# A recurrent attention and gated feed-forward kernel: another way to build the mask, the block sums and the first transposed x in its setup

## The chip, the cores and the metric

The kernel runs on one core of a Trainium2 chip. The core has five engines that run side by side and wait for each other through semaphores: TensorE (PE, matrix products into PSUM), VectorE (DVE), ScalarE (ACT), GpSimd (POOL) and SyncE (SP, which here only issues transfers). The metric is the device time of one execution in microseconds, as a median of runs.

## The reference

x is [8, 1024, 512] in float32. With xn the layer norm of x over its last axis, the result is `x + s * silu(g)`.

- s is a recurrent attention. q = xn Wq; for i in 0 to 2, k = xn Wk[i], v = xn Wv[i], scores = (q kT) * w, where w[t, s] = sigmoid(decay_logits[i]) ** max(s - t - 1, 0) for s > t and 0 elsewhere; the three results (scores v) are blended with softmax(xn Wg), and go through Wo, times out_scale.
- g is a feed-forward net, silu(gate) * up and a product with down, whose three weight matrices (1376 x 512, 1376 x 512, 512 x 1376) are given as a table of 16 values and, for each weight, an index into it.

## The kernel before

**Numbers.** Each float32 operand of a matrix product is split in two float16 halves, high and low; a product takes three matmuls (high x high, high x low, low x high). The gate and up products use a scheme of seven products of sub-blocks in place of eight (Strassen's, in Winograd's form): it needs the sums S1 to S4 of sub-blocks of the weights and T1 to T4 of sub-blocks of the transposed x.

**Setup, and then a loop.** The setup turns the indices into weights, 33 units of 128 x 512 weights (`UNITS`). A unit b goes through these hands:

- POOL casts its codes to float16 in memory (L613, L618); SP loads them, each code row to four groups of partitions (L517).
- DVE compares them with the four candidates of its partition, 4 instructions of 128 x 2048 (L999), a one-hot matrix. It may be three units ahead of PE.
- PE looks up (`look_up`, L1371): 8 groups of 4 small matmuls, high and low half, into PSUM.
- ACT stores both halves as float16 (`store`, L761).

Behind its look-up, PE works through the unit's **pieces** (`PIECES`, `add_up`, `take_high`): a block sum is made in a PSUM bank by four matmuls of 512 columns with the identity or its negative (`plus`, `minus`; a high, a low, b high, b low). ACT copies the bank out as the high half (`store_sum`), PE subtracts this copy in the bank (one matmul, a unit later), and ACT copies what is left as the low half. The order of pieces is a table by units: for a set of blocks that begins at unit `BASE[s]`, S1 at +2 and +3, S3 at +3 and +4, S2 at +4 and +5, S4 at +6 and +7; T1 to T4 at units 26 to 31. Finished blocks of the weights are written to memory (`write_block`).

Between the units other setup work is placed by tables as well: the squares, high halves and low halves of the attention weights (`SQUARE_AT`, `HIGH_AT`, `LOW_AT`), where ACT makes a high half and DVE the low half from it (`low_part`, L1010); the norm and the normalized tiles of the first 512 rows of x (`XHAT_AT`, `XLOW_AT`); and their four transposes, which SP issues as DMA transposes at units 22, 23, 25 and 26 (`XPOSE_AT`, L498).

**The decay mask.** POOL raises the three decays to 128 powers, one per partition (L663), writes them with a row of zeros to a table in memory (L666, L668), and reads the table back, each partition one value further on (L670). PE turns the rows about with a product by a flip matrix (L1416), and ACT copies the outcome out of PSUM with its scale (L833). `mask` shares its memory with `eye4`, which DVE needs at the start.

The setup ends when PE has waited for the last piece, the low halves and the mask (L1584 to L1587). The loop then takes 16 groups of 512 rows: q and k (L1429), v, 42 sub-block products (L1541) with scores and retrieval between them, the down product (L1570), and the output. DVE combines the sub-block products (`u2` L1251, `c12` L1273 and others).

## Time and profile before

| | |
|---|---|
| median of 3 runs | 1888.74 us (1886.42 to 1889.11) |
| the profiled execution | 1886.13 us, its span in the profile 1884.3 us |
| granted TensorE clock | 0.996 of full speed |
| busy: PE, DVE, ACT, POOL | 1841.1, 1226.4, 648.9, 644.1 us |
| first matmul of the loop (L1429) | 144.4 us |
| chain that ended last | PE 94% |

The profile is of one execution. A line such as L1371 is a line of the kernel before, printed above. Matmuls overlap, so the start of one to the start of the next is what one costs; the duration shown is longer. In rows in order of time the figures are the start and the time until the last of the merged instructions ends, and what stands in brackets is how long the engine was idle before and which engine and line released it.

### The profile page before, as it was taken

How to read it: one execution, taken by the hardware profiler on the slowest of the kernel's cores; microseconds unless marked ns; L12 is line 12 of the kernel's file. 1: busy time of each engine (PE TensorE's matmuls, PEld its weight loads, DVE VectorE, ACT ScalarE, POOL GpSimd, SP SyncE). 2: the span in 40 equal slices, each digit the busy share in tenths (PEclk: the TensorE clock that was granted, in tenths of full speed). 3: DMA queues.
4: the chain of work that ended last, by engine and by line, in shares of the span. 5: the costliest groups of instructions: out<-in, count | busy, mean ns of one | idle time of the engine just before them, and what ended most of it. 6: DMA issues, size and time to landing. Idle time of an engine off the chain costs nothing.

```text
span 1884.3 us, 39423 instructions
## 1 busy us (share of the span) xinstructions
PE 1841.1 (98%) x14198; PEld 1249.3 (66%) x14198; DVE 1226.4 (65%) x2565; ACT 648.9 (34%) x1168; POOL 644.1 (34%) x642
## 2 busy tenths in 40 slices
PE   5889999999999999999999999999999999999999
PEld 1236758486776848576685858667584867758485
DVE  7785848485674848576584847658484856748374
ACT  2564324242333414233342324233242424334131
POOL 9301606043250605234160613416061432506021
PEclk9999999999999999999999999999999999999999
DMA  9974737465563736566472655548363655737350
GB/s 216 312 219 135 186 87 184 103 162 135 149 168 102 199 84 163 132 159 153 111 198 78 172 133 153 142 128 193 82 176 113 161 139 139 178 96 198 68 141 26
DMA packets 353020, 276.73 MB, mean 147 GB/s; under 512 B 220349, under 2 KB 257600, under 8 KB 352752
## 3 DMA queue, kind: packets, MB, share of 16 engines
q1 hardware_dynamic: 341888, 267.61, 54.4%
q0 software_dynamic: 10944, 6.50, 2.4%
q8 instruction: 132, 2.16, 0.4%
q14 instruction: 56, 0.46, 0.1%
HBM read 204.16 MB, written 30.54 MB: 125 GB/s over the span
## 4 chain that ended last, share of the span: by engine, by line
PE 94%; DVE 1%; SPq 1%; ACT 1%; POOL 1%; DMA 1%; issue 1%; another core or an unknown queue 0%; POOLq 0%; DVEq 0%
PE F L1541 43%; PE F L1570 24%; PE B L1429 16%; PE B L1461 2%; PE B L1434 2%; PE B L1436 2%; PE B L1435 2%; DVE region L999 1%; PE F L1371 1%; POOL codes L613 1%; PE F L1434 1%; PE F L1435 1%; PE F L1436 1%; DMA region<-in_wv 1%; SPq L517 0%
## 5 line engine op out<-in xcount | busy, mean ns | idle before, releaser
L1541 PE MATMUL F<-xtc,ring 128*128 128x256 f16 (+1 forms) x4224 | 497.7, 273 | 0.0
L1541 PEld LDWEIGHTS F<-xtc,ring 128*128 128x128 f16 (+1 forms) x4224 | 416.0, 100 | 42.4
L1570 PE MATMUL F<-wd_hi,region 128*128 128x512 f16 (+1 forms) x1408 | 429.2, 379 | 0.0
L1541 PE MATMUL F<-xt,ring 128*128 128x256 f16 (+1 forms) x3168 | 378.8, 273 | 0.1
L1541 PEld LDWEIGHTS F<-xt,ring 128*128 128x128 f16 (+1 forms) x3168 | 310.0, 100 | 35.7 <-DVE region L1261 1.8
L1570 PE MATMUL F<-wd_lo,region 128*128 128x512 f16 (+1 forms) x704 | 266.7, 379 | 0.0
L1570 PEld LDWEIGHTS F<-wd_hi,region 128*128 128x128 f16 (+1 forms) x1408 | 137.6, 98 | 162.6
L1345 DVE SCALAR_TENSOR_TENSOR region<-F,row_out,region 128x512 f32<-128x512 f32 x64 | 48.0, 751 | 291.3 <-ACT region L926 291.3
L680 POOL TENSOR_TENSOR rstd<-var,nhalf 128x4 f32<-128x4 f32 x15 | 15.1, 1008 | 638.1 <-DVE var L957 638.1
L686 POOL TENSOR_TENSOR region<-region 128x512 f16<-128x512 f32 x96 | 121.7, 1267 | 220.8 <-ACT region L761 220.8
L926 ACT ACTIVATE region<-F,scale_hf 128x512 f32<-128x512 f32 x64 | 44.0, 687 | 435.6 <-PE F L1570 435.6
L761 ACT ACTIVATE region<-region 128x512 f16<-128x512 f32 x192 | 113.7, 592 | 138.8 <-DVE region L1293 105.6
L1429 PE MATMUL B<-xt,a_hi 128*128 128x512 f16 x512 | 154.6, 382 | 4.3 <-issue 3.0
L698 POOL TENSOR_TENSOR region<-faded,region 128x384 f16<-128x384 f32 x64 | 69.5, 1086 | 226.7 <-ACT region L761 226.7
L1222 DVE SCALAR_TENSOR_TENSOR region<-B,region 128x512 f16<-128x512 f32 x64 | 44.2, 691 | 134.6 <-ACT region L761 134.6
L1429 PE MATMUL B<-a_hi,xt 128*128 128x387 f16 x512 | 128.7, 328 | 0.0
L874 ACT ACTIVATE region<-F,scale_down 128x512 f32<-128x512 f32 x96 | 62.2, 648 | 186.9 <-POOL region L693 126.9
L1570 PEld LDWEIGHTS F<-wd_lo,region 128*128 128x128 f16 (+1 forms) x704 | 68.9, 98 | 79.5
L693 POOL TENSOR_TENSOR region<-region 128x512 f16<-128x512 f32 x96 | 103.0, 1073 | 24.5 <-ACT region L761 24.5
L761 ACT ACTIVATE region<-B 128x512 f16<-128x512 f32 (+1 forms) x128 | 68.7, 536 | 110.5 <-PE B L1429 110.5
L1251 DVE TENSOR_TENSOR region<-F,region 128x512 f32<-128x512 f32 x96 | 61.7, 643 | 66.7 <-PE F L1541 56.5
L1436 PE MATMUL B<-region 128*128 128x128 f16 x552 | 99.0, 219 | 0.0
(197 smaller groups left out, 2955.4 us busy)
## 6 DMA issues: line engine op xcount, KB each, us to landing
ring<-blocks SPq DMA_DIRECT2D x546, 256.0 KB, 3.1
x_sb<-in_x SPq DMA_DIRECT2D x64, 256.0 KB, 3.5
out_y<-x_sb SPq DMA_DIRECT2D x64, 256.0 KB, 2.0
ring<-blocks SPq DMA_DIRECT2D x112, 128.0 KB, 2.5
blocks<-ring SPq DMA_DIRECT2D x35, 256.0 KB, 6.0
x_sb<-codes SPq DMA_DIRECT2D x10, 512.0 KB, 8.0
chalf<-codes SPq DMA_DIRECT2D x9, 512.0 KB, 8.2
xt<-codes SPq DMA_DIRECT2D x9, 512.0 KB, 9.6
```

Of the source, the lines that this page charges most:

```text
L686: G_.tensor_tensor(h_lo[0:M, ms, 0:HALF], XC[s % 2][0:M, 0:w], h_hi[0:M, ms, 0:HALF], ALU.subtract).then_inc(s_hl1, 1)
L693: G_.tensor_tensor(h_lo[0:M, ms, HALF:GRP], SC[0:M, 0:w], h_hi[0:M, ms, HALF:GRP], ALU.subtract).then_inc(s_hl2, 1)
L698: G_.tensor_tensor(pr_half[:, 1], probs[:, :], pr_half[:, 0], ALU.subtract).then_inc(s_prl, 1)
L761: return nc.scalar.activation(dst, src, ACT.Copy, **kw)
L874: nc.scalar.activation(SC[0:M, 0:w], pair(0, s), ACT.Silu, scale=f_down[0:M, LUT:LUT + 1]).then_inc(s_sg1, 1)
L1251: V_.tensor_tensor(xc, pair(1, s), xc, ALU.add).then_inc(s_u2, 1)
L1429: ins = T_.matmul(bank[0:M, 0:cols], a, b, start=(n == 0), stop=(n == 3 * len(pairs) - 1))
L1434: T_.matmul(out, ah, bh, start=True, stop=False)
L1435: T_.matmul(out, ah, bl, start=False, stop=False)
L1436: return T_.matmul(out, al, bh, start=False, stop=True)
L1541: ins = T_.matmul(out_, a, b, start=fresh, stop=False, skip_group_check=True)
L1570: ins = T_.matmul(bf[:, :], a, b, start=(k == 0 and n == 0), stop=(k == FC - 1 and n == 2))
```

## The change

- **Mask.** The flip matrix, the table in memory and its three transfers, PE's product and ACT's copy are gone. POOL makes the mask in place: an iota of s - t - 1, a maximum with 0, a power of the decays, a select that keeps s > t, and a product with the scale, each over 3 x 128 columns and each waiting for the one before.
- **Block sums.** S2, S4, T2 and T4 start from what the bank still holds. After `take_high` that is the low half of the sum before; one matmul adds its high half again, and two add the other block. S4 and T2 have the opposite sign of before, so `u2` and `c12` subtract the product where they added it. Each set's S1, S2 and S4 now share one of two banks; S3 has a third; x and the T sums have the fourth.
- **First x.** Each tile of the first 512 rows is transposed on PE, 4 matmuls of 128 columns against `plus` per half, and copied out by ACT; these are pieces of units 15 to 22. SP's four DMA transposes are gone. T1, T2, T4, T3 come at units 23, 25, 27 and 29.
- **Low halves.** `LOW_AT` puts DVE's low halves at units 23, 25, 26, 28 and 30; the high halves stay at 19, 21, 22, 24 and 26.

```diff
--- before.py
+++ after.py
@@ -106,32 +106,38 @@
-    SUM = {S1: (A21, 1, A22), S3: (A11, -1, A21), S2: (S1, -1, A11), S4: (A12, -1, S2)}
-    SUMT = {T1: ("B12", "B11"), T3: ("B22", "B12"), T2: ("B22", T1), T4: ("B21", T2)}
-    BANK_OF = {S1: 0, S2: 1, S3: 2, S4: 3}
-    BANK_OFT = {T1: 0, T2: 1, T3: 2, T4: 3}
...
+    SUM = {S1: (A21, 1, A22), S3: (A11, -1, A21), S2: (S1, -1, A11), S4: (S2, -1, A12)}
+    SUMT = {T1: ("B12", -1, "B11"), T3: ("B22", -1, "B12"), T2: (T1, -1, "B22"), T4: (T2, 1, "B21")}
+    CHAINED = (S2, S4)
+    CHAINEDT = (T2, T4)
...
-    q = BASE[SETS[-2]]
-    for op, a in ((T1, 4), (T3, 5), (T2, 6), (T4, 8)):
-        PIECES.setdefault(q + a, []).append((None, op, 0))
-        PIECES.setdefault(q + a + 1, []).append((None, op, 1))
+    for op, u in ((T1, 23), (T2, 25), (T4, 27), (T3, 29)):
+        PIECES.setdefault(u, []).append((None, op, 0))
+        PIECES.setdefault(u + 1, []).append((None, op, 1))
+    for j, u in enumerate((15, 17, 19, 21)):
+        PIECES.setdefault(u, []).append(("x", j, 0))
+        PIECES.setdefault(u + 1, []).append(("x", j, 1))
...
+    def bank_of(s, op):
+        if s is None or s == "x":
+            return 3
+        return 2 if op == S3 else SETS.index(s) % 2
...
-        bank = (BANK_OFT if s is None else BANK_OF)[op]
-        if part == 0:
-            BUSY[s, op] = before.get(bank, 0)
-        else:
-            before[bank] = n + 1
+        BUSY[s, op, part] = before.get(bank_of(s, op), 0)
+        before[bank_of(s, op)] = n + 1
@@ -434,14 +435,13 @@
-        LOW_AT = {20: 0, 22: 1, 23: 2, 25: 3, 27: WO}
+        LOW_AT = {23: 0, 25: 1, 26: 2, 28: 3, 30: WO}
...
-        XPOSE_AT = {22: 0, 23: 1, 25: 2, 26: 3}
@@ -531,8 +533,6 @@
-                if b in XPOSE_AT:
-                    transpose_x(0, XPOSE_AT[b], XPOSE_AT[b] + 1)
@@ -620,16 +620,12 @@
-            G_.memset(flip[:, :], 0.0).then_inc(s_cstep, 1)
...
-            G_.memset(fade_end, 0.0).then_inc(s_cstep, 1)
...
-            pool.wait_ge(s_cstep, 6)
+            pool.wait_ge(s_cstep, 4)
...
-            G_.affine_select(out=flip[:, :], in_=flip[:, :], compare_op=ALU.not_equal, fill=1.0,
-                             base=-(P - 1), pattern=[[1, P]], channel_multiplier=1).then_inc(s_const, 1)
@@ -658,16 +654,24 @@
-            pool.wait_ge(s_cstep, 9)
+            pool.wait_ge(s_cstep, 7)
...
-            with nc.allow_non_contiguous_dma(reason="384 values, once"):
-                pool.dma_start(fade_rows[:, P:2 * P], fade_end).then_inc(s_row, 16)
-                pool.wait_ge(s_pow, 1)
-                pool.dma_start(fade_rows[:, 0:P].rearrange("h t -> t h"), fade_t[:, :]).then_inc(s_row, 16)
-                pool.wait_ge(s_row, 32)
-                pool.dma_start(mask_up[:, :, :], bass.AP(fade_rows, 1, [[1, P], [2 * P, NH], [1, P]])).then_inc(s_mrow, 16)
...
+            band = dict(pattern=[[0, NH], [-1, P]], base=-1, channel_multiplier=1)
+            G_.iota(mask_up, allow_small_or_imprecise_dtypes=True, **band).then_inc(s_mstep, 1)
+            pool.wait_ge(s_mstep, 1)
+            G_.tensor_scalar(mask_up, mask_up, 0.0, None, ALU.max).then_inc(s_mstep, 1)
+            pool.wait_ge(s_mstep, 2)
+            pool.wait_ge(s_pick, 2 * CG)
+            G_.tensor_tensor(mask[:, :, :], decay[:, :].unsqueeze(2).broadcast_to([P, NH, P]), mask_up,
+                             ALU.pow).then_inc(s_mstep, 1)
+            pool.wait_ge(s_mstep, 3)
+            G_.affine_select(out=mask[:, :, :], in_=mask[:, :, :], compare_op=ALU.is_ge, fill=0.0,
+                             **band).then_inc(s_mstep, 1)
+            pool.wait_ge(s_mstep, 4)
+            G_.tensor_scalar(mask[:, :, :], mask[:, :, :], 2.0 ** SP, None, ALU.mult).then_inc(s_mask, 1)
@@ -717,9 +721,9 @@
-                    G_.tensor_tensor(tt[:, T2], b22, tt[:, T1], ALU.subtract).then_inc(s_tt, 1)
+                    G_.tensor_tensor(tt[:, T2], tt[:, T1], b22, ALU.subtract).then_inc(s_tt, 1)
...
-                    G_.tensor_tensor(tt[:, T4], b21, tt[:, T2], ALU.subtract).then_inc(s_tt, 1)
+                    G_.tensor_tensor(tt[:, T4], b21, tt[:, T2], ALU.add).then_inc(s_tt, 1)
@@ -818,20 +822,21 @@
-                if s is None:
-                    copy(held(s, op, part), B[BANK_OFT[op]][:, :].rearrange("p (k t) -> p k t", k=2)).then_inc(s_sum, 1)
+                bank = B[bank_of(s, op)]
+                if s == "x":
+                    t = TILES[op]
+                    copy(xt[:, 0, part * KC:(part + 1) * KC, t * P:(t + 1) * P],
+                         bank[:, :].rearrange("p (k t) -> p k t", k=KC)).then_inc(s_sum, 1)
+                elif s is None:
+                    copy(held(s, op, part), bank[:, :].rearrange("p (k t) -> p k t", k=2)).then_inc(s_sum, 1)
...
-                    copy(held(s, op, part), B[BANK_OF[op]][:, 0:width(s)]).then_inc(s_sum, 1)
+                    copy(held(s, op, part), bank[:, 0:width(s)]).then_inc(s_sum, 1)
...
-                if b == NU - 1:
-                    act.wait_ge(s_pmask, 1)
-                    copy(mask[:, :, :].rearrange("p h t -> p (h t)"), LUHI[NU % 2][:, 0:HD],
-                         scale=2.0 ** SP).then_inc(s_mask, 1)
@@ -1248,7 +1253,7 @@
-                    V_.tensor_tensor(xc, pair(1, s), xc, ALU.add).then_inc(s_u2, 1)
+                    V_.tensor_tensor(xc, xc, pair(1, s), ALU.subtract).then_inc(s_u2, 1)
@@ -1270,7 +1275,7 @@
-                    V_.tensor_tensor(YC[0:M, 0:w], pair(3, s), YC[0:M, 0:w], ALU.add).then_inc(s_c12, 1)
+                    V_.tensor_tensor(YC[0:M, 0:w], YC[0:M, 0:w], pair(3, s), ALU.subtract).then_inc(s_c12, 1)
@@ -1383,40 +1387,49 @@
-                if s is None:
-                    (a, b), sign, bank = SUMT[op], -1, B[BANK_OFT[op]][:, :]
-                else:
-                    a, sign, b = SUM[op]
-                    bank = B[BANK_OF[op]][:, 0:width(s)]
-                if BUSY[s, op]:
-                    pe.wait_ge(s_sum, BUSY[s, op])
+                a, sign, b = (SUMT if s is None else SUM)[op]
+                bank = B[bank_of(s, op)][:, :] if s is None else B[bank_of(s, op)][:, 0:width(s)]
+                if BUSY[s, op, 0]:
+                    pe.wait_ge(s_sum, BUSY[s, op, 0])
...
-                T_.matmul(bank, plus[:, :], held(s, a, 0), start=True, stop=False)
-                T_.matmul(bank, plus[:, :], held(s, a, 1), start=False, stop=False)
-                T_.matmul(bank, other[:, :], held(s, b, 0), start=False, stop=False)
-                T_.matmul(bank, other[:, :], held(s, b, 1), start=False, stop=True).then_inc(s_psum, 1)
+                if op in (CHAINEDT if s is None else CHAINED):
+                    T_.matmul(bank, plus[:, :], held(s, a, 0), start=False, stop=False, skip_group_check=True)
+                else:
+                    T_.matmul(bank, plus[:, :], held(s, a, 0), start=True, stop=False, skip_group_check=True)
+                    T_.matmul(bank, plus[:, :], held(s, a, 1), start=False, stop=False, skip_group_check=True)
+                T_.matmul(bank, other[:, :], held(s, b, 0), start=False, stop=False, skip_group_check=True)
+                T_.matmul(bank, other[:, :], held(s, b, 1), start=False, stop=True,
+                          skip_group_check=True).then_inc(s_psum, 1)
...
-                bank = B[BANK_OFT[op]][:, :] if s is None else B[BANK_OF[op]][:, 0:width(s)]
+                bank = B[bank_of(s, op)][:, :] if s is None else B[bank_of(s, op)][:, 0:width(s)]
...
+            def turn_x(j, hl):
...
+                bank = B[bank_of("x", j)]
+                if BUSY["x", j, hl]:
+                    pe.wait_ge(s_sum, BUSY["x", j, hl])
+                pe.wait_ge(s_xlo, j + 1)
+                for k in range(KC):
+                    ins = T_.matmul(bank[:, k * P:(k + 1) * P], xhat_half[:, TILES[j], hl, k * P:(k + 1) * P],
+                                    plus[:, :], start=True, stop=True, skip_group_check=True)
+                ins.then_inc(s_psum, 1)
...
-                if b == NU - 1:
-                    pe.wait_ge(s_mrow, 16)
-                    pe.wait_ge(s_wst, STORED[NU - 2])
-                    T_.matmul(LUHI[NU % 2][:, 0:HD], flip[:, :], mask_up.rearrange("p h t -> p (h t)"),
-                              start=True, stop=True).then_inc(s_pmask, 1)
...
-                    if part == 0:
+                    if s == "x":
+                        turn_x(op, part)
+                    elif part == 0:
@@ -1481,7 +1494,7 @@
-                    pe.wait_ge(s_xt[t], 16 * (gi + 1))
+                    pe.wait_ge(s_xt[t], 16 * (gi + FREE))
```

## Rows read from the trace of the kernel before

**Rows 1.** The page, part 1: busy time by engine
```profile
PE 1841.1 (98%) x14198; PEld 1249.3 (66%) x14198; DVE 1226.4 (65%) x2565; ACT 648.9 (34%) x1168; POOL 644.1 (34%) x642
```

**Rows 2.** The chain that ended last, in order of time: start us, us, what
```profile
6.89 13.96 POOL codes L613 x20
...
62.77 0.43 PE B L1396
...
111.40 0.22 PE B L1396
...
144.36 20.13 PE B L1429 x96
```

**Rows 3.** PE in order of time (start us, us), first matmuls of some look-ups
```profile
88.35 0.40 PE L1371 MATMUL F<-region,pick_hi 128*32 128x512 f16 x4 [1.17 <-DVE region L999]
...
91.97 0.40 PE L1371 MATMUL F<-region,pick_hi 128*32 128x512 f16 x4
...
95.19 0.40 PE L1371 MATMUL F<-region,pick_hi 128*32 128x512 f16 x4
...
98.81 0.40 PE L1371 MATMUL F<-region,pick_hi 128*32 128x512 f16 x4
...
103.94 0.62 PE L1371 MATMUL F<-region,pick_hi 128*32 128x512 f16 x4 [2.89 <-ACT tt L761]
...
108.57 0.40 PE L1371 MATMUL F<-region,pick_hi 128*32 128x512 f16 x4 [0.31 <-ACT ring L761]
...
112.20 0.40 PE L1371 MATMUL F<-region,pick_hi 128*32 128x512 f16 x4
...
136.88 0.40 PE L1371 MATMUL F<-region,pick_hi 128*32 128x512 f16 x4
...
138.72 0.91 PE L1416 MATMUL F<-faded,mixed 128*128 128x384 f32 x2
```

**Rows 4.** DVE in order of time: a compare (L999), low halves (L1010)
```profile
90.10 2.85 DVE L999 TENSOR_SCALAR region<-xt,code 128x2048 f16<-128x2048 f16 x4
...
93.62 0.76 DVE L1010 SCALAR_TENSOR_TENSOR a_lo<-region,scale_up,a_hi 128x512 f16<-128x512 f32 x1 [0.67 <-ACT a_hi L761]
...
101.31 1.82 DVE L1010 SCALAR_TENSOR_TENSOR a_lo<-region,scale_up,a_hi 128x1536 f16<-128x1536 f32 x1 [1.63 <-issue]
```

**Rows 5.** ACT in order of time, around unit 21 and at the end
```profile
99.67 1.60 ACT L761 ACTIVATE a_hi<-region,scale_up 128x1536 f16<-128x1536 f32 x1
...
139.91 0.53 ACT L761 ACTIVATE mask<-F 128x384 f32<-128x384 f32 x1
...
140.28 0.65 ACT L761 ACTIVATE ring<-B 128x512 f16<-128x512 f32 x1
```

**Rows 6.** PE's matmuls of 128 columns (168 us), then SyncE's queue (93 us)
```profile
168.40 0.22 PE L1434 MATMUL B<-region 128*128 128x128 f16 x1
...
168.85 0.22 PE L1436 MATMUL B<-region 128*128 128x128 f16 x1
...
93.69 9.60 SPq L498 DMA_TRANSPOSE xt<-xhat_half  x1
```

**Rows 7.** POOL in order of time, setup
```profile
5.03 0.29 POOL L631 TENSOR_SCALAR_AFFINE_SELECT mixed<-mixed 128x128 f32<-128x128 f32 x1
...
84.80 0.77 POOL L655 IOTA fade_s<- 128x3 f32 x1 [8.03 <-issue]
...
87.74 1.17 POOL L663 TENSOR_TENSOR fade_tile<-decay,fade_tile 128x3 f32<-128x3 f32 x1
```

**Rows 8.** Lines by themselves: duration ns min/median/max, first and last start us, forms
```profile
L680 POOL TENSOR_TENSOR rstd<-var,nhalf x15: 1006/1007/1029, 161.2 to 1679.3; 128x4 f32<-128x4 f32 x15
...
L703 POOL TENSOR_TENSOR faded<-state,fade_tile x56: 825/827/1157, 173.2 to 1831.7; 128x384 f32<-128x384 f32 x56
...
L999 DVE TENSOR_SCALAR region<-x_sb,code x1: 748/748/748, 88.1 to 88.1; 128x2048 f16<-128x2048 f16 x1
...
L1286 DVE SCALAR_TENSOR_TENSOR region<-region,scale_hf x96: 480/752/1716, 175.1 to 1848.7; 128x512 f32<-128x512 f32 x80, 96x256 f32<-96x256 f32 x16
```

More of the change, by code:

```diff
@@ L189, in attention_ffn_kernel @@
         fade_s = sb("fade_s", [P, NH], F32)
-        flip = mixed
-        fade_end = mask[0:NH, 1]
-        fade_rows = nc.dram_tensor("fade_rows", [NH, 2 * P], F32, kind="Internal")
         codes16 = nc.dram_tensor("codes16", [NU, QR, CG * BANK], F16, kind="Internal")
@@ L324, in attention_ffn_kernel @@
         s_pick = sem("pick_ready")
-        s_row = sem("fade_rows_written")
-        s_mrow = sem("mask_rows_in")
-        s_pmask = sem("mask_in_psum")
+        s_mstep = sem("mask_step")
         s_mask = sem("mask_ready")
@@ L474, in _ @@
             sp.sem_inc(s_xtc, 32 * FREE)
+            for t in range(GT):
+                sp.sem_inc(s_xt[t], 16 * FREE)
             sp.dma_start(lutrow[:, :], lut.partition_broadcast(P)).then_inc(s_small, 16)
@@ L1039, in shifted @@
                 V_.tensor_scalar(dst, src, 23, None, ALU.logical_shift_left).then_inc(done, 1)
-            dve.wait_ge(s_const, 3)
+            dve.wait_ge(s_const, 2)
             step(V_.tensor_reduce(eye[:, :], eye4.rearrange("p a c -> p c a"), AX.X, ALU.add))
@@ L1376, in ready @@
                 if s is None and op not in SUMT:
-                    for t in range(GT):
-                        pe.wait_ge(s_xt[t], 16)
+                    pe.wait_ge(s_sum, NTH["x", GT - 1, 1] + 1)
                 elif (s, op) in HELD:
```

## The prediction

> **What bounds the kernel now.** I read the page first: PE is busy 98% of the span [rows 1], so a stage gets shorter only where PE waits or does less. The chain of waits, in order of time, splits the span in two. It begins on POOL, which issues the code casts, and up to 144.36 us it passes through several engines. From there on it is PE's matmuls of the main loop [rows 2]. The change edits the setup; in the loop it only swaps operands and signs. So I price the 144.4 us of setup and let the rest shift with it.
>
> PE's instructions in order of time say where the setup can give. A unit (one look-up and its pieces) starts with the first L1371 matmul. From unit 25 to unit 32 PE takes 112.20 to 136.88 = 24.68 us for 7 units with 50 matmuls of 512 columns (pieces of units 25 to 31 by the old table) [rows 3]. An add costs 0.216 us at full clock [rows 2], so 24.68 - 50 x 0.216 leaves 1.98 us for a look-up with its gaps. There PE sets the pace. Units 20 to 24, started at 91.97, 95.19, 98.81, 103.94 and 108.57 and ended at 112.20, have 5, 5, 1, 4 and 5 such matmuls. At PE's pace they would take 3.06, 3.06, 2.20, 2.84 and 3.06; they took 3.22, 3.62, 5.13, 4.63 and 3.63. The excess is 0.16 + 0.56 + 2.93 + 1.79 + 0.57 = 6.0 us. The DVE rows name its cause: the low half of matrix 0 stands 0.67 us idle for ACT's high half. That of matrix 1 starts at 101.31 after 1.63 us idle, just as ACT's high half of it ends (99.67 + 1.60 = 101.27) [rows 4, 5]. The compare of unit 23 is queued behind this 1.82 us instruction, and PE's look-up 23 stands 2.89 us idle (put down to ACT, but its one-hots are what is late). It then restarts with matmuls of 0.62 instead of 0.40 us, TensorE at 1.2 instead of 2.4 GHz [rows 3].
>
> **Low halves four units behind.** The same five DVE instructions, now at units 23, 25, 26, 28 and 30. ACT has finished each high half over one unit before. Nothing waits, so DVE starts compare 21 at 92.95 instead of after the low half of matrix 0 (93.62 + 0.76), and what PE then sees late is nothing: PE's own pace takes over. This returns the 6.0 us. DVE needs 2.65 us a compare (its 2.85 for four overlap by about 0.2), PE 1.98 plus its pieces. With my new piece counts DVE stays ahead by 0.8 us at its closest, unit 27, after both 1.7 us low halves. If that lead were gone, each us of DVE delay would cost one.
>
> **Chained sums.** S2, S4, T2 and T4 lose one matmul each: 140 become 126, 14 in all. Units 20 to 31 go from 70 to 63 (T moved forward within them): 7 x 0.216 = 1.5 us. One more lies in unit 11, at half clock, on the chain: 0.43 [rows 2]; I take 0.4. Those of earlier units stand in waits for codes, and cost and give nothing. S4 in the tail is counted below. The loop's two DVE subtractions have the shape and length of the adds they replace; their second operand is now in PSUM, which no row shows. As PE is the loop's bound, I take 0, bounds -1 to +3 us.
>
> **First x on TensorE.** Added: 8 pieces of 4 matmuls of 128 columns at units 15 to 22, and 8 ACT copies of about half a us. From 168.40 to 168.85 eight such matmuls follow each other in 0.45: 0.056 each [rows 6]. In units 15 to 18 PE waits for DVE anyhow. In 19 to 22 there are 16: 0.9 us. ACT gets 0.5 us more a unit and its two 1.6 us high halves fall in units 21 and 22, so PE's T1 and S4 pieces meet it about 0.3 us early: -0.3. Removed: four DMA transposes. The longest holds SyncE's queue 9.60 us [rows 6], with code loads and block writes behind it; but the idle times of DVE after 61 us end on ACT and not on codes, so it gives 0 (bounds 0 to 1). The Trainium skill (TensorE: Matmul & The Clock Gate, Part 4: PE-mode transpose) has such a transpose at about 275 ns in a kernel; by it 16 of them would be 4.4 us and not 0.9, a gain 3.5 us smaller. The rows above are for ordinary matmuls against an identity, which these are, so I keep 0.056.
>
> **Mask, what goes.** On POOL a memset and a select for the flip matrix (0.29 for the select [rows 7]) and a small memset, 0.5 us in all ahead of the casts that start the chain. DMA sets the pace soon after: 0.3, bounds 0 to 0.5. At the end, ACT's copy of the mask: the next copy starts 0.37 later (139.91 to 140.28) [rows 5], plus one matmul of S4, 0.22: 0.6 us. PE's mask matmul (at 138.72) lies beside ACT's stores.
>
> **Mask, what comes.** Five POOL instructions over 384 columns after the small powers, from about 88.9 us (87.74 + 1.17 [rows 7]). Four are simple. A select of 128 columns takes 0.29, a product of 384 columns 0.83 [rows 7, 8]: 1.2 to 3.3 us, I take 2.3. Do they hold DVE? A POOL iota of three columns started at 84.80 and took 0.77, to about the end of a compare: one engine does wait for the other. In the loop the DVE line L1286 runs 0.75 us as a rule and 1.72 at most, beside POOL [rows 8]. So I charge 2.3 less the 0.8 of DVE lead: 1.5, bounds 0 to 3.3. The power itself no row shows at this size. Below: 0.83, the product of the same shape. Above: 1.007 us for 4 columns [rows 8] is 0.25 a column, x 384 = 97 us. Three columns took 1.17 against 1.007 for four [rows 7, 8], so a fixed part is large; I take the geometric middle, 9 us. As to what it holds: the compare at 88.1 ran its usual 748 ns inside the power of 87.74 to 88.91 [rows 7, 8]. So I let it hold nothing. It ends near 100, and the mask is wanted only by the loop at about 138.
>
> The Trainium skill (SBUF — State Buffer, Who interferes with whom) says that a DVE instruction in a two-port mode and a GpSimd instruction exclude each other, and that the one issued first has the ports to its end. The 0.77 us iota agrees, the compare inside the power doesn't; by the rule DVE would also stand still for the whole power.
>
> **Sum.** 6.0 + 1.5 - 0.9 - 0.3 = 6.3 for units 19 to 32; + 0.4 + 0.3 + 0.6 - 1.5 = 6.1 us. The loop would start at 138.3 instead of 144.36. The profiled execution took 1886.1 (span 1884.3); less 6.1 is 1880.0. The median of the runs before, 1888.7, is 2.6 above that execution, so I forecast 1882.6.
>
> **Rivals.** (1) The power of 384 columns sets the end. If it holds the ports for its length P, each us of P costs one, and the change is slower than before from P = 6.1. At my 9 us it is 1882.6 + 9 = 1891.6, with PE's restart at half clock about 1893. If it holds nothing but is slow, the mask comes at 91.2 + P, late from P = 47; at 97 the loop starts at 188 and the time is near 1933. For it: the stretched DVE line, and four columns that cost 1.007. Against: the undisturbed compare, and little growth from three to four columns. 0.27. The page's rule is this rival.
> (2) The wait moves and does not go. ACT carries 8 copies more just where its long high halves lie, POOL's simple instructions cost the full 3.3, the 0.7 of the early stages stay hidden, and half of the 6.0 comes back as PE waits: 6.1 - 1.8 - 0.7 - 3.0 = 0.6, time 1888.1. For it: ACT's 1.60 us halves at units 21 and 22. Against: ACT is idle ahead of most of its stores. 0.17.
> (3) The forecast, 0.56, own range 1879.5 to 1885: all savings in full (0.2 + 0.2 more), POOL free (1.5 more) and 1 us for spread at the low end; 1.8 for POOL at 3.3 and some ACT at the high.
>
> **Numbers.** Below 0.2% (3.8 us) a measurement of this kernel can't tell a change from none. The forecast case is faster nearly always (0.55), and 0.03 comes from cases between it and rival 2; the rest of 2 is no change, 0.15. Rival 1 is slower, 0.27. Range: from 1879 up to 1895, which leaves out the long powers.
>
> **What would show it.** Right: the first L1429 at about 138; no idle of PE over 1 us and no matmuls at half clock between units 19 and 32; compares 20 to 23 back to back. DVE's compares at 0.75 us each beside POOL's power; a power under 40 us. Wrong: compares stretched to the length of a POOL instruction (rival 1), or a first L1429 that waits on POOL; ACT named ahead of PE's pieces of units 23 and 24 (rival 2); and a loop that isn't 1740 us long (1884.3 - 144.4), which none of my terms has.

## The result: slower by 0.4%, and one GpSimd instruction has it

The kernel before took 1888.92 us (median of 6 runs, 1886.42 to 1890.11), the changed kernel 1895.38 us (6 runs, 1894.83 to 1898.36): ratio 1.0038, 95% interval 1.0025 to 1.0051. The forecast was 1882.6 us, faster. The second case of rival 1, a power that holds (almost) nothing but is slow, is what happened, with 62 us instead of my 9.

The page of the changed kernel, part 1 (answers to [rows 1]): POOL is busy 62.6 us longer, PE 4 us less.

```profile
PE 1837.0 (97%) x14214; PEld 1249.3 (66%) x14214; DVE 1227.0 (65%) x2565; ACT 652.1 (34%) x1175; POOL 706.7 (37%) x641
```

The chain of waits, in order of time (answers to [rows 2]): POOL stands alone on it from 91.88 on, and the loop starts 12.1 us later than before.

```profile
91.88 61.88 POOL mask L668
156.46 20.08 PE B L1442 x96
```

POOL's instructions in order of time (start us, us), answering to [rows 7]. The power of 384 columns takes 61.87 us; the iota, the maximum, the select and the product around it take 1.03, 1.71, 0.53 and 1.21.

```profile
87.82 1.17 POOL L659 TENSOR_TENSOR fade_tile<-decay,fade_tile 128x3 f32<-128x3 f32 x1
88.96 1.03 POOL L663 IOTA faded<- 128x384 f32 x1
90.09 1.71 POOL L665 TENSOR_SCALAR faded<-faded 128x384 f32<-128x384 f32 x1
91.88 61.87 POOL L668 TENSOR_TENSOR mask<-decay,faded 128x384 f32<-128x384 f32 x1
153.81 0.53 POOL L671 TENSOR_SCALAR_AFFINE_SELECT mask<-mask 128x384 f32<-128x384 f32 x1
154.43 1.21 POOL L674 TENSOR_SCALAR mask<-mask 128x384 f32<-128x384 f32 x1
```

PE's instructions in order of time (answers to [rows 3]; idle time and releaser in brackets). After unit 19's first look-up (88.43) PE is idle only 0.31 us (for DVE, at 90.59) and 0.21 us (for ACT, at 103.78) until the tail; the 2.89 us hole and the half clock behind it are gone. The last two steps of the tail start at 134.98 and 136.48, and then PE stands 19.59 us for the mask.

```profile
88.43 0.40 PE L1376 MATMUL F<-region,pick_hi 128*32 128x512 f16 x4 [1.16 <-DVE region L1004]
...
134.98 0.38 PE L1398 MATMUL B<-ring,plus 128*128 128x512 f16 x1 [1.53 <-ACT ring L765]
...
136.48 0.39 PE L1410 MATMUL B<-ring,minus 128*128 128x512 f16 x1 [0.69 <-ACT ring L765]
...
156.46 1.03 PE L1442 MATMUL B<-xt,a_hi 128*128 128x512 f16 x2 [19.59 <-POOL mask L674]
```

In every kernel here the loop's first matmul, where the mask doesn't hold it, comes 1.57 to 1.82 us after that last one-matmul step (1.57 before, 142.79 to 144.36). Without the wait it would have come at 136.48 + 1.57 = 138.05, or up to 0.25 later.

DVE's instructions in order of time (answers to [rows 4]). The low halves stand without idle time. Four compares that end beside the iota took 3.01 and the next eight 6.42; further into the power eight take 5.38. One by one, the usual compare takes 0.75; the one beside the iota took 1.02, the two beside the maximum 0.98 each, and the first one that begins inside the power 1.31, which is the row of 92.26 (from the same view of a narrower stretch).

```profile
87.53 3.01 DVE L1004 TENSOR_SCALAR region<-x_sb,code 128x2048 f16<-128x2048 f16 x4
90.46 6.42 DVE L1004 TENSOR_SCALAR region<-xt,code 128x2048 f16<-128x2048 f16 x8
...
92.26 1.31 DVE L1004 TENSOR_SCALAR region<-xt,code 128x2048 f16<-128x2048 f16 x1
...
96.80 5.38 DVE L1004 TENSOR_SCALAR region<-chalf,code 128x2048 f16<-128x2048 f16 x8
102.10 0.75 DVE L1015 SCALAR_TENSOR_TENSOR a_lo<-region,scale_up,a_hi 128x512 f16<-128x512 f32 x1
102.76 5.38 DVE L1004 TENSOR_SCALAR region<-x_sb,code 128x2048 f16<-128x2048 f16 x8
108.06 1.81 DVE L1015 SCALAR_TENSOR_TENSOR a_lo<-region,scale_up,a_hi 128x1536 f16<-128x1536 f32 x1
```

The account between the two profiled executions: the start goes from 144.36 to 156.46, +12.1 us; the loop (span less start) from 1884.3 - 144.4 = 1739.9 to 1893.2 - 156.5 = 1736.7, -3.2 us. Together +8.9, the difference of the spans; the medians differ by 6.5.

**A mark behind the noisy part.** Everything ahead of unit 19 shifts as a block from execution to execution: its first look-up started anywhere from 88.04 to 91.02. So starts are compared below by their *distance*: the time from that look-up to the loop's first matmul. Two executions of one kernel (e4 and e12 below) give 48.77 and 48.79, though the starts themselves are 138.69 and 137.85. All distances come from one profiled execution per kernel, so these two are the whole measure of their spread, beside e3, which adds only GpSimd work to the kernel before and gives 55.88 against 56.01. Before it is 144.36 - 88.35 = 56.01; after, without the mask's wait, 138.05 - 88.43 = 49.62.

### The profile page after: what moved, and what is told of

It reads as the page before. It is cut to its first block, busy times and chain, and to the rows that moved or that the text cites. A ratio compares the mean times of both kernels' runs of the same rounds, so it can differ in the third digit from the quotient of the medians.

```text
span 1893.2 us, 39454 instructions
## 1 busy us (share of the span) xinstructions
PE 1837.0 (97%) x14214; PEld 1249.3 (66%) x14214; DVE 1227.0 (65%) x2565; ACT 652.1 (34%) x1175; POOL 706.7 (37%) x641
## 4 chain that ended last, share of the span: by engine, by line
PE 92%; POOL 4%; DVE 1%; DMA 1%; issue 1%; SPq 1%; ACT 1%; POOLq 0%; DVEq 0%
PE F L1554 43%; PE F L1583 24%; PE B L1442 16%; POOL mask L668 3%; PE B L1474 2%; PE B L1447 2%; PE B L1449 2%; PE B L1448 2%; DVE region L1004 1%; PE F L1447 1%; PE F L1448 1%; PE F L1449 1%; DMA region<-in_wv 1%; SPq L519 0%; DMA lutrow<-in_lut 0%
## 5 line engine op out<-in xcount | busy, mean ns | idle before, releaser
L1256 DVE TENSOR_TENSOR region<-region,F 128x512 f32<-128x512 f32 x96 | 61.4, 640 | 66.6 <-PE F L1554 56.5
L1442 PEld LDWEIGHTS B<-xt,a_hi 128*128 128x128 f16 x512 | 49.8, 98 | 83.0 <-issue 24.8
```

The lines of the kernel that those rows point to most:

```text
L1256: V_.tensor_tensor(xc, xc, pair(1, s), ALU.subtract).then_inc(s_u2, 1)
L1442: ins = T_.matmul(bank[0:M, 0:cols], a, b, start=(n == 0), stop=(n == 3 * len(pairs) - 1))
```

## The experiments

Ratios are to the kernel before on the same chip, with 95% intervals.

**e1: the change with the old mask** (the memory table, flip matrix, TensorE matmul and ACT copy put back; everything else as after).

```
- G_.tensor_tensor(mask, decay broadcast, mask_up, ALU.pow)
...
+ pool.dma_start(fade_rows[:, 0:P].rearrange("h t -> t h"), fade_t)
...
+ T_.matmul(LUHI[NU % 2][:, 0:HD], flip, mask_up)
+ copy(mask, LUHI[NU % 2][:, 0:HD], scale=2.0 ** SP)
```

> The changed kernel with the mask of the kernel before put back (flip matrix, table in memory, PE product, ACT copy); chained sums, first x on TensorE and the late low halves stay. Theory: POOL's power over 384 columns (61.9 us in the profile after) is the whole loss, and the rest of the change gives what was forecast. Then PE, whose last setup matmul of the profile after ended near 137, starts the loop at 138 to 139 us instead of 144.4, and the time is 5 to 8 us below before (ratio 0.9960 to 0.9975). Rival: the 19.6 us wait for the mask hides another loss (first transposed x late, block writes late, ACT behind); then the loop starts after 141 us and the ratio is 0.999 or more.

Measured 1882.32 us, ratio 0.9972 (0.9962 to 0.9983). So the loss sits in the mask, as the theory has it. But the loop started at 142.59 and not at 138 to 139, as the rival has it (its ratio did not come); the distance is 53.24, 4.5 us more than the factored mask of e4 gives. 0.4 of it lies in the tail, where the mask's matmul and copy stand: from unit 32's first look-up to the loop 7.22 us pass here and 6.83 in e4. The other 4.3 lie in units 22 and 23. PE's instructions with idle time in front, between 99 and 111 us, show most of these: 0.39 + 0.21 + 0.78 + 1.65 = 3.0 us in which PE stood, mostly for nothing that the profile shows.

```profile
100.70 0.38 PE L1382 MATMUL F<-region,pick_hi 128*32 128x512 f16 x1 [0.39 <-issue]
101.28 0.42 PE L1382 MATMUL F<-region,pick_hi 128*32 128x512 f16 x2 [0.21 <-issue]
103.56 0.39 PE L1416 MATMUL B<-ring,minus 128*128 128x512 f16 x1 [0.78 <-ACT ring L767]
106.63 0.40 PE L1382 MATMUL F<-region,pick_lo 128*32 128x512 f16 x3 [1.65 <-issue]
```

ACT, in order of time, stands there too, and again no engine or transfer of the kernel is named.

```profile
101.44 0.60 ACT L767 ACTIVATE wd_hi<-F 128x512 f16<-128x512 f32 x1 [3.72 <-remote]
```

**e2: the kernel before with GpSimd's mask only.**

```
- the table's three DMAs, the flip matmul and the ACT copy
+ iota, maximum, power of 384 columns, select, product on GpSimd
```

> The kernel before with the mask made on POOL and nothing else of the change. Theory (the power alone loses): the power takes 61 to 63 us, the loop starts at 155 to 157 us, 11 to 13 us later than before. The loop of the changed kernel was 3 us shorter than before (1736.7 against 1739.9 us). If that comes from the two DVE subtractions or the x sums, this loop is 1740 us long and the ratio 1.006; if it comes from the late start or is chance, it may be 1737 here too, ratio 1.0045. Rival: the power is slow only beside the new order of compares; then it is clearly off 62 us here.

1898.89 us, ratio 1.0059 (1.0044 to 1.0075); the loop starts at 158.89. POOL in order of time:

```profile
94.47 61.86 POOL L662 TENSOR_TENSOR mask<-decay,faded 128x384 f32<-128x384 f32 x1
156.40 0.53 POOL L665 TENSOR_SCALAR_AFFINE_SELECT mask<-mask 128x384 f32<-128x384 f32 x1
```

The mask edit alone makes the kernel slower. The power took the same 61.86 us, and the first compare inside it again 1.31. The loop was 1738.2 us long. The start is 2 us later than I expected because the whole setup was (unit 19 at 91.02).

**e3: powers of several sizes**, added to the kernel before on GpSimd behind its table: 24 and 96 columns with exponents up to 31, 96 columns with exponent 1, the same once more when DVE is done, and a product of 96 columns.

> The kernel before with POOL powers added after its mask table is read, where POOL is idle: 24 columns, 96 columns with exponents 0 to 31, 96 columns with all exponents 1, and, once DVE has ended its setup, 96 columns again and a product of 96 columns. The added results are not used. Theory (own arithmetic, about 0.16 us a column over a fixed part of about 0.4): 4.2, 15.8, 15.8, 15.8 us, and under 0.6 us for the product. Rival 1 (POOL and DVE share ports and the power fights the compares): the power beside an idle DVE is far shorter, under 5 us. Rival 2 (the cost hangs on the exponents): with exponents of 1 it is under half of that with 0 to 31.

1886.36 us (one run). POOL in order of time; x2 groups the 24 with the first 96, and the two later 96.

```profile
102.23 20.67 POOL L680 TENSOR_TENSOR probe_o<-decay,probe_e 128x24 f32<-128x24 f32 x2
...
123.64 31.70 POOL L680 TENSOR_TENSOR probe_o<-decay,probe_e 128x96 f32<-128x96 f32 x2
155.42 0.35 POOL L692 TENSOR_TENSOR probe_o<-decay,probe_e 128x96 f32<-128x96 f32 x1
```

Line L680 by itself (duration ns min/median/max) gives the ends of the range:

```profile
L680 POOL TENSOR_TENSOR probe_o<-decay,probe_e x4: 4680/15761/15942, 102.2 to 139.7; 128x96 f32<-128x96 f32 x3, 128x24 f32<-128x24 f32 x1
```

24 columns take 4.68 us; 96 take 15.91 with exponents up to 31, 15.94 with exponent 1, and 15.62 when DVE is idle for the first 9.9 us of it (it has four short instructions in the rest). (15.91 - 4.68) / 72 = 0.156 us a column, and (61.87 - 15.91) / 288 = 0.160 from there to 384. In these runs the price is linear in the columns, with under 1 us fixed, and neither the exponent nor DVE's work moves it by more than 0.4 us. A product of 96 columns takes 0.35: the power is over 45 times that.

**e4: the change with a factored mask.** Each decay's power of an exponent is a product of a coarse, a fine and a row power: 8 + 16 + 1 columns for each of 3 decays, 75 in all instead of 384, made on GpSimd ahead of its all-reduce, where it is idle.

```
...
+ G_.tensor_tensor(powers, decay broadcast, powers, ALU.pow)          # 75 columns
...
+ G_.tensor_tensor(coarse(mask_up), powers 8 broadcast, powers 16 broadcast, ALU.mult)
+ G_.tensor_tensor(mask, mask_up, powers 1 broadcast, ALU.mult)
+ G_.affine_select(out=mask, in_=mask, compare_op=ALU.is_ge, fill=0.0)
```

> The changed kernel with the mask factored: powers of 8, 16 and 1 columns for each decay (75 columns in one instruction), two products of 384 columns and a select, on POOL between the code casts and the sum over partitions, where it stood idle 21 us. Theory (0.16 us a column): the power takes 12 to 13 us, the mask is ready near 72 us, the sum over partitions is hardly later, and the loop starts at 137.5 to 138.5 us: 6 to 8 us below before, and equal to or up to 1 us better than with the table put back. Rival (a fixed cost dominates the power or POOL's work holds DVE): the power takes over 20 us or compares are stretched, the sum over partitions comes late, and the loop starts after 141 us.

1876.95 us, ratio 0.9944 (0.9931 to 0.9958); the loop starts at 138.69. This beats both kernels: 11 us under the one before, of which 7.2 are the shorter distance (56.01 to 48.77) and 3.8 a shorter loop (1739.9 to 1736.1), which no edit to the loop explains (see there below). Run again as e12:

> The kernel with the factored mask once more, as it was, to stand beside the other three on the same chip: ratio 0.994 to 0.995 as measured (0.9944), loop start at 138 to 139.5, loop 1736 to 1737 us long. If the loop's start or length moves by 2 us or more between two executions of one kernel, then differences of that size between single profiles say nothing.

1876.91 us, ratio 0.9938 (0.9925 to 0.9952), loop start 137.85, loop 1736.95 us long. POOL in order of time in e12: 12.32 us for 75 columns (0.164 a column; up to 15.29 in its other variants, 0.204 a column, for which I have no cause), and the mask is ready at 71.9, 66 us ahead of need.

```profile
55.72 12.32 POOL L664 TENSOR_TENSOR powers<-decay,powers 128x75 f32<-128x75 f32 x1 [0.15 <-POOL powers L660]
68.14 0.95 POOL L667 TENSOR_SCALAR powers<-powers 128x3 f32<-128x3 f32 x1
68.48 1.28 POOL L669 TENSOR_TENSOR faded<-powers 128x384 f32<-128x384 f32 x1
69.83 1.16 POOL L674 TENSOR_TENSOR mask<-faded,powers 128x384 f32<-128x384 f32 x1
71.07 0.86 POOL L677 TENSOR_SCALAR_AFFINE_SELECT mask<-mask 128x384 f32<-128x384 f32 x1
```

**e7: e4 with the low halves at their old units**, which prices that item.

```
- LOW_AT = {23: 0, 25: 1, 26: 2, 28: 3, 30: WO}
+ LOW_AT = {20: 0, 22: 1, 23: 2, 25: 3, 27: WO}
```

> The factored-mask version of the changed kernel with the low halves back at units 20, 22, 23, 25 and 27. The prediction gave this edit 6.0 us (PE's excess in units 20 to 24). Theory (it holds): the loop starts 4 to 6 us later than 138.7, at 143 to 145. Rival (part of the 6.0 us was the stall that the table in memory caused in the same units): it starts 1 to 3 us later, at 140 to 142.

1883.95 us, ratio 0.9978 (0.9969 to 0.9987), which is 6.4 us more than e4's by the ratios. The distance is 145.96 - 89.92 = 56.04, 7.3 us more than e4's and more than the 4 to 6 that I expected. It is also the distance of the kernel before (56.01): without the later low halves, all the other edits together bring nothing behind unit 19. DVE in order of time: its four idle times on ACT's high halves are back, 1.27, 2.12, 1.38 and 1.79 us. In the kernel before they were 0.67, 1.63, 0.37 and 1.50, and ACT's high half of matrix 1 started 11.32 us behind unit 19's first look-up (99.67 - 88.35); here it starts 12.28 us behind it (102.20 - 89.92). ACT has the copies of x in front of them here, so part of the 7.3 us is probably a wait that the x edit lengthens; no run separates it. PE in order of time has its hole on DVE again, as before.

```profile
95.67 0.76 DVE L1033 SCALAR_TENSOR_TENSOR a_lo<-region,scale_up,a_hi 128x512 f16<-128x512 f32 x1 [1.27 <-ACT a_hi L783]
...
103.84 1.82 DVE L1033 SCALAR_TENSOR_TENSOR a_lo<-region,scale_up,a_hi 128x1536 f16<-128x1536 f32 x1 [2.12 <-ACT a_hi L783]
...
116.72 0.24 DVE L1033 SCALAR_TENSOR_TENSOR a_lo<-region,scale_up,a_hi 128x12 f16<-128x12 f32 x1 [1.38 <-ACT a_hi L783]
...
124.05 0.75 DVE L1033 SCALAR_TENSOR_TENSOR wo_lo<-q,scale_up,wo_hi 128x512 f16<-128x512 f32 x1 [1.79 <-ACT wo_hi L783]
```

```profile
106.47 0.40 PE L1394 MATMUL F<-region,pick_hi 128*32 128x512 f16 x4 [3.15 <-DVE region L1022]
```

**e6: the kernel before with the low halves moved only.**

> The kernel before with one edit: the low halves of the weights four units behind the high ones. My theory: the item is worth the 6.0 us of its term wherever it stands, so ratio 0.996 to 0.998 (1881.5 to 1885 beside 1888.5), the loop starts at 138 to 141, and VectorE's idle before its low halves (0.67 and 1.63 and more in the kernel before) is gone. Rival: with the table still in memory, part of the late start of the run with the old mask comes back (its loop began at 142.6), and the edit alone is worth 2 us or less: loop start at 142 or later, ratio 0.999 or more.

1884.34 us, ratio 0.9975 (0.9965 to 0.9985). Alone, beside the table and the DMA transposes, the item is worth less: the distance is 142.79 - 90.70 = 52.09, 3.9 us under before, between the two expectations (6.0, and 2 or less); the ratio is in the theory's range, the start in the rival's. PE and DVE in order of time show part of what took its place: PE stands 0.88 and 0.49 us for nothing visible, and DVE 0.31 and 0.55 for late code blocks.

```profile
103.82 0.41 PE L1371 MATMUL F<-region,pick_hi 128*32 128x512 f16 x2 [0.88 <-issue]
```

```profile
111.28 2.74 DVE L999 TENSOR_SCALAR region<-xt,code 128x2048 f16<-128x2048 f16 x4 [0.31 <-DMA xt<-codes]
...
116.30 2.74 DVE L999 TENSOR_SCALAR region<-xt,code 128x2048 f16<-128x2048 f16 x4 [0.55 <-DMA xt<-codes]
```

**e8: e4 without chained sums.**

```
- CHAINED = (S2, S4)      CHAINEDT = (T2, T4)
+ CHAINED = ()            CHAINEDT = ()
```

> The kernel with the factored mask, with S2, S4, T2 and T4 built from two held blocks again (four first matmuls instead of three, and one more copy term), all else the same. My theory: one matmul of 512 columns more per chained sum, 1.9 us of TensorE by the terms of the forecast (1.5 in units 20 to 31, 0.4 in unit 11), so the loop starts 1 to 2 us later than in the same kernel with chained sums run beside it, ratio to it 1.0005 to 1.001. Rival: TensorE waits for ScalarE's or VectorE's copies in these units anyway, and the start moves by less than 0.5 us.

1878.63 us, ratio 0.9948 (0.9935 to 0.9961). The distance is 138.47 - 88.37 = 50.10, 1.3 us more than e12's. The intervals overlap, so the median's 1.7 us alone would show nothing; the distance, as far as one profile of each goes, does.

**e9: e4 with the first x transposed by DMA** again.

> The factored-mask version of the changed kernel with the first x transposed by the four DMA transposes of before (at their old places in SyncE's queue; T sums stay at units 23 to 30). Theory (prediction: the DMA transposes cost nothing, the TensorE ones 0.9 us and ACT 0.3): the loop starts within 1.3 us of 138.7, rather earlier. Rival 1 (the DMA transposes hold the DMA engines, and instructions and stores wait behind them, as with the table): it starts at 141 or later. Rival 2: T1 at unit 23 waits for the last transpose, PE idle there, 1 to 4 us.

1879.23 us, ratio 0.9950 (0.9937 to 0.9964). The distance is 139.12 - 90.80 = 48.32: TensorE's transposes cost 0.5 us against DMA's. Neither rival showed: the start is under 141, and PE is idle only 0.16 us in unit 23, for a block sum's copy by ACT and not for T1. The loop was 1739.5 us long, 3.4 more than e4's, and nothing in this edit touches it.

**e5: the kernel before with the factored mask only.**

> The kernel before with the factored mask made on POOL ahead of the sum over partitions, and nothing else of the change. Theory (the table in memory cost about 4 us, since the loop starts at 142.6 us with the table put back and at 138.7 with the factored mask): the loop starts at 140 to 141.5 instead of 144.4 us, ratio 0.9970 to 0.9985. Rival (the table's stall lies beside DVE's waits for ACT in the kernel before and costs nothing there): only the tail's 0.5 us goes, start 143.5 to 144, ratio 0.9990 or more.

1884.61 us, ratio 0.9986 (0.9977 to 0.9995). The loop starts at 145.73 and not at 140 to 141.5; the distance is 145.73 - 90.11 = 55.62, 0.4 us under before. So the theory that the table costs 4 us fails in this kernel, and the rival's 0.5 us fits the distance. The ratio, at the edge between the two, owes the rest of its gain to a loop of 1736.6 us.

**e10 and e11: does the table's traffic hold the other queues?** e10 is e4 with the scattered write of the small powers (4 bytes each), e11 is e4 with the whole table, written and read, used by nobody.

```
+ pool.dma_start(fade_rows[:, 0:P].rearrange("h t -> t h"), fade_t)     # e10, e11
+ pool.dma_start(table, bass.AP(fade_rows, 1, [[1, P], [2 * P, NH], [1, P]]))   # e11: 192 KB
```

> The factored-mask version of the changed kernel plus one transfer: POOL writes the 384 small powers to memory, 4 bytes at a time, where the table was written; nothing reads them. Theory (this scattered write is what made the table cost about 4 us, by holding up the other transfers near 95 to 101 us, instruction loads among them): the loop starts at 141.5 to 143 us, DMA moves under 100 GB/s in 94 to 100 us, and the ratio to before is 0.996 to 0.998. Rival (the table's read or PE's and ACT's part in it cost the 4 us): the loop starts at 138.5 to 139.5 and the ratio is about 0.9945.

> The kernel with the factored mask, and beside it the old table, complete (the row write, the scattered write of 4-byte values, the read of 192 KB into a tile of its own), which nothing uses and nobody but GpSimd waits for. Theory A (the table's transfers hold the other queues' writes and reads): the stretch of 94 to 103 us shows under 70 GB/s as in the kernel with the old table, blocks land in 12 us instead of 5, and the loop starts 2 to 4 us later than in the same kernel without the table run beside it. Theory B (the late start of the run with the old table was its setup's own variation, or the wait for the last row): no change beyond 1 us, and over 100 GB/s in that stretch.

e10: 1875.73 us, ratio 0.9941 (0.9927 to 0.9954), distance 136.83 - 88.04 = 48.79, that of e12. The theory fails: DMA moved 181, 122 and 141 GB/s in the stretches from 94 to 103 us, less than the 283, 308 and 282 without the write but not under 100, and the start didn't move. e11: 1877.22 us, ratio 0.9943 (0.9930 to 0.9956), distance 137.09 - 88.11 = 48.98. Busy time by stretch (PE, PEld, DVE, ACT, POOL, then granted clock, DMA share and GB/s), e11 first, e12 second:

```profile
94.00:97.00 3.00, 3.00 (x41) 1.28 (x39) 3.00 (x6) 2.47 (x5) 0.00 (x0) 1.00 1.94 173
97.00:100.00 3.00, 3.00 (x44) 1.38 (x40) 3.00 (x6) 2.83 (x6) 0.00 (x0) 1.00 0.46 40
100.00:103.00 3.00, 2.80 (x43) 1.26 (x40) 3.00 (x6) 3.00 (x6) 0.00 (x0) 1.00 1.05 110
```

```profile
94.00:97.00 3.00, 3.00 (x41) 1.28 (x37) 3.00 (x6) 2.92 (x7) 0.00 (x0) 1.00 0.82 283
97.00:100.00 3.00, 3.00 (x44) 1.37 (x40) 3.00 (x5) 2.31 (x5) 0.00 (x0) 1.00 1.00 308
100.00:103.00 3.00, 3.00 (x57) 1.40 (x49) 3.00 (x6) 3.00 (x6) 0.00 (x0) 1.00 0.98 282
```

Theory A's first half holds: with the table all transfers together sink to 40 GB/s in one stretch of 3 us, and to 173 and 110 in the two around it, where they else run at about 300, and blocks land in 11.4 us in the median instead of 5.5. Its second half doesn't: the engines work through (PE loses 0.2 us), and the loop starts 0.2 us later. So this traffic doesn't by itself hold PE and ACT as they were held in e1, and PE in e6.

The DMA view shows one thing that sets e1 and e6 apart. From 87 to 104 us, every other kernel here has at least one load of instructions on queue q8, at 94.1 to 98.2 us; e1 and e6 have none, and get theirs at 104.3 and 104.4. In e11 the load came at 94.1, just ahead of the slow stretch. The rows are those of e11 for 87 to 104 us and of e1 for 104 to 106 us (packets, MB, share of 16 engines):

```profile
q8 instruction: 1, 0.02, 0.3%
```

```profile
q8 instruction: 1, 0.02, 3.0%
```

That fits engines that stand for their own code, because a load falls due while the table's traffic is slow. It is a correlation in 14 profiles: the view doesn't say which engine a load is for, and no run moves a load by itself. So e11 doesn't clear the traffic either.

## Why the prediction was wrong

**The step that failed** is "I take the geometric middle, 9 us" in the mask's part. The term was 9 us and measured 61.87. I had the right upper row (1.007 us for four columns, so up to 97 us) and argued it down because three columns took no less than four [rows 8]. That growth was no evidence: two rows a column apart, with 0.16 us expected between them and other instructions overlapping both, can't separate a fixed part from a slope. From 24 and 96 columns the slope is 0.156, and 4 x 0.16 is 0.64 of the 1.007. My own condition, late from P = 47, was then met: the loop starts 18.4 us later than its matmuls' other inputs allow (156.46 - 138.05). By 91.2 + P the mask would have been ready at 153.1; it was at 155.64 (154.43 + 1.21), since POOL's four simple instructions took 4.5 us where I had 2.3 and at most 3.3. Of the signs that I had named for a wrong forecast, two came: a first loop matmul that waits on POOL, and a loop that isn't 1740 us long; a power under 40 us, a sign of being right, did not.

**That the power holds nothing** was right but for its start. The first compare that begins inside it takes 1.31 us instead of 0.75 (92.26; 1.31 in e2 too); after that eight compares take 5.38 us as usual, as long as DVE has any, to 131 us. The rule of the Trainium skill (SBUF — State Buffer, Who interferes with whom), that a DVE instruction in a two-port mode and a GpSimd instruction exclude each other for their length, is borne out in part by the compares beside the iota and the maximum, which are stretched to 1.02 and 0.98 us, and not by those beside the power.

**Simple GpSimd instructions hold DVE**: forecast 1.5 us of loss. The eight compares of 90.46 took 6.42 instead of 5.38, and the four before 3.01 instead of 2.73: 1.3 us, 0.7 of it beside the iota and the maximum and 0.6 at the start of the power. The distance shows 49.62 - 48.79 = 0.8 of it against e12, where nothing of this stands beside these compares.

**Low halves**: forecast 6.0; 7.3 by e7 against e4, 3.9 by e6 against before. The mechanism is right (the 2.89 us hole and DVE's idle times go with this edit and come back without it, 3.15 us in e7), the size depends on the rest: 1.3 over the forecast or 2.1 under it. Which of the other edits makes the difference is not shown; e6's own rows show PE and DVE standing for other things, and e7's show ACT later.

**Chained sums**: forecast 1.9, of which 1.5 behind unit 19; measured 1.3 there, which includes S4's matmul in the tail (0.22 in the forecast's 0.6).

**First x on TensorE**: forecast -1.2; measured -0.5. PE in order of time in the changed kernel has a piece of four transposes at 95.06 and the next instruction at 95.28: 0.22 us for the four, as the rows had it.

```profile
95.06 0.39 PE L1420 MATMUL B<-plus,xhat_half 128*128 128x128 f16 x4
95.28 0.38 PE L1400 MATMUL B<-ring,plus 128*128 128x512 f16 x1
```

The page "TensorE: Matmul & The Clock Gate", Part 4: PE-mode transpose, of the Trainium skill, has about 275 ns for a transpose in the transpose mode, from which 4.4 us for 16 is an estimate. These are ordinary matmuls against an identity, and the measurement speaks for the rows.

**Mask, what goes**: forecast 0.6 in the tail (0.37 for ACT's copy, 0.22 for S4's matmul) and 0.3 early. e5, which has the copy's part alone, shows 0.4 behind unit 19; the early part can't be told from the spread of the block ahead of it.

**The sum without the power**: forecast start 138.3, possible 138.05. By distances 5.4 was forecast (6.3 + 0.6 - 1.5) and 6.4 measured (56.01 - 49.62). That the sum came within 1.0 us is in part luck: the single terms are off by up to 1.3 us in the kernel with all edits, both ways, and they don't add up (measured singly, 7.3 for the low halves, 1.3 for the chained sums, -0.5 for x and 0.4 for the old mask make 8.5, and together in e12 they are 7.2).

**The loop**: forecast 0, and 3.2 us shorter. No edit to the loop explains it. The length goes with PE's idle time that is put down to issue in the loop: 3.0, 3.4, 3.7 and 2.3 us in before, e3, e6 and e9 (lengths 1739.9, 1740.6, 1741.1, 1739.5), and 0 to 1.3 us in all the others (1736.1 to 1738.2). e5 has the old adds and a short loop, e9 the new subtractions and a long one, so the subtractions are cleared. The waits for issue are one row each in the waits of PE, here of before and after (us in total, times, longest):

```profile
PE B L1429 <- issue: 3.0, 9, 0.5
```

```profile
PE B L1442 <- issue: 0.7, 3, 0.3
```

They are not spread over the loop. The program repeats its code for two groups of rows (a pass) and jumps back, some 216 us apart. All 45 such waits of the 14 profiles stand at a pass's first matmul after a jump, or 2.5 to 3.3 us behind it; none stands at the start of a pass's second group. Instruction loads crowd there too: in the kernel before, queue q8 brings 3 in the 10 us around the jump at 1013.5 us, and 13 in the 207 us that follow:

```profile
q8 instruction: 3, 0.05, 2.0%
```

```profile
q8 instruction: 13, 0.21, 0.4%
```

The waits 2.5 to 3.3 us behind the jump occur in three kernels only, before, e3 and e6, and these three share PE's program. e5 and e2, whose PE program lacks only the mask's matmul, have none of these and loops of 1736.6 and 1738.2 us. e9, without the x pieces in PE's program, has its long waits, 1.18 and 0.95 us, at the jump itself. So the loop's 3 us look like PE waiting for its code behind the jump, by an amount that hangs on how long its program ahead of the loop is. That is argued and not tested; the test would be the kernel before with a few idle instructions of PE ahead of the loop. It is worth 3 us, half of what the change as a whole was forecast to bring, and the forecast had nothing for it.

## What to carry to other kernels

Before elementwise work moves to an engine, look for its price per column at a size of the same order; where only a row of a few columns exists, take the linear end as the forecast's own case if the step then decides the sign. A slow function over a structured grid can be factored (75 powers and two products for 384 powers), and an instruction whose inputs are there early belongs where its engine is idle, not where its result is wanted. And compare starts from a mark behind the noisy part: two executions of one kernel agreed to 0.02 us from unit 19, and only to 0.8 us in absolute time. A gain that is read off one pair of kernels holds for that pair: the same edit was worth 7.3 us in one and 3.9 in the other.

## What the hardware showed that I had not expected

- A GpSimd power costs 0.16 us a column of 128 partitions (up to 0.20 in some runs of 75 columns), 61.87 us for 384 columns. It stretches the first compare of DVE inside it from 0.75 to 1.31 us (to 0.84 with 96 columns in e3) and leaves the rest at their 0.67 us pace; an iota and a maximum of the same 384 columns take 1.03 and 1.71 us and stretch the three compares beside them by 0.7 us in all.
- A table's round trip through memory brought all transfers down to 40 GB/s for 3 us and to 110 to 173 around it, and cost the loop's start 0.2 us in e11. In e1 and e6, where an instruction load came 10 us later than in e11, PE and ACT stood for nothing that the profile names: in e1, ACT 3.72 us in one piece and PE 2.25 us in three.
- PE loses 0 to 3.7 us a run to idle times that all stand within 3.3 us of the loop's jumps back, where instruction loads crowd, and that differ between kernels whose loops are the same.
